# Second attention of a fused transformer kernel: value products of three steps a block divided in two, three buffers of probabilities

## The chip, the cores and the metric

One core of one Trainium2 chip runs the whole program in one launch. The metric is device time in microseconds (us). Five engines matter: TensorE (PE; its weight loads are shown as PEld), VectorE (DVE), ScalarE (ACT), GpSimd (POOL) and SyncE (SP), which issues most of the DMAs. Each runs its own list of instructions in order and meets the others only at semaphores.

## The reference, cut to what matters

The input x is 16 sequences of 256 tokens with 128 features. Four layers follow each other, each on the layer norm of x and each added to x: an attention with 2 heads, a gated feed-forward, a second attention with 16 heads of 8 features, and the same feed-forward again. The change is in the second attention:

```python
qkv = encodings @ attn_w.T + attn_b            # 16 heads, 8 features each
scores = einsum('bhki,bhqi->bhkq', k, q) / math.sqrt(8)
scores = where(mask, scores, -10000.0)         # a key is seen by itself and later queries
probs = softmax(scores, axis=2)                # over the keys
combined = einsum('bhkq,bhkl->bhql', probs, v)
out = combined.transpose(...).reshape(b, n, 128) @ out_w.T + out_b
```

## The kernel before

**Blocks and steps.** The second attention goes through 8 blocks of 2 sequences (512 tokens). A block has 8 steps (`STEPS`, L1300); step n handles one sequence (n % 2) and one group of 4 heads (n // 2). The 4 heads are two pairs, p = 0 and p = 1. Blocks 1 to 4 are the two rounds of a loop whose semaphore targets stand in registers (`run_inner`, L256); blocks 0, 5, 6 and 7 are written out.

**Two passes over the scores.** For block b+1 a first pass (`pe_first`, L1339) makes the scores with queries on the partitions, and DVE takes the row maximum of each (`dve_first`, L1665). The maxima are transposed on PE (`pe_maxT`, L1360), copied and negated on ACT (`act_max`, L1580) and carried by a DMA from the ACT queue into the operand rows of the queries (`act_max_rows`, L1586). For block b a second pass (`pe_second`, L1373) makes the scores with keys on the partitions, the maximum already taken off, and leaves them in one pair of PSUM banks for both pairs of heads. ACT takes the exponential out of these banks into a buffer of probabilities in SBUF (`act_exp`, L1563), POOL zeroes the masked half of the diagonal tiles (`pool_mask`, L1781), and the value products (`pe_values`, L1393) multiply the probabilities by the values, 16 columns of weights a head (8 values and a column of ones that sums the denominator), the 4 heads in four column strips of the array.

**The value products of a step.** There are two key tiles. Key tile 0 (kc = 0) meets all 256 queries, key tile 1 (kc = 1) only the last 128, and accumulates on them. In fp32 each product is two passes on PE, so a step has 8 passes of 256 columns and 8 of 128.

**The order on PE, step n** (`pe_step`, L1424): second pass of pair 0; first pass of pair 1 of block b+1, which ends in two mask products (L1357); a small piece of other work (`pe_between`, L1464); second pass of pair 1; first pass of pair 0; value products of step n−1. Below, the part from the second pass of pair 0 is the step's A half and the part from the second pass of pair 1 its B half; each begins by waiting until ACT has emptied the two banks (semaphore `s_ex`). The small pieces are: step 0 `pe_maxT` of the block's upper half, step 1 the transposes of the layer norm, 2 and 3 the q and k projections of block b+2, 4 and 5 half of the v projection each, 6 `pe_maxT` of the next block's lower half, 7 the output projection of block b−1, which waits for POOL's normalisation (L1792).

**Buffers of probabilities.** There are two, used in turn (`prob[n % 2]`). ACT waits before the exponential of step n until the value products of step n−2 are done (`s_pv`, L1569).

**Order on ACT:** exponential of pair 0; `act_max` at steps 0 and 6; exponential of pair 1; at steps 0, 2, 4, 6 the copy of the output bank (`act_out`, L1574), which waits for the value products of the odd step before.

**The loads of the rows.** The q and k of block b+2 go through DRAM. SP (`sp_body`, L1893) stores the q rows, then the reciprocals of the denominators that DVE makes at the end of step 3 (`dve_inverse`, L1682), then the k rows; once these have landed it issues the load of the lower half of the rows (L1866), which the first pass of step 0 of the next block waits for (L1344). The second pass of step 0 waits for the DMA of the maxima (L1428).

Of the kernel before, what the change touches and what calls it, by code (L numbers as in the profile page):

```python
# [24 lines left out]
P = 128  # L25
B, T, E = 16, 256, 128
# [17 lines left out]
GROUPS = 4  # L44
QUART = P // GROUPS
# [35 lines left out]
def is_block(b, t):  # L81

    return isinstance(b.t, int) and b.t == t


def build(nc, io):
    ctx = ExitStack()
    with ctx:
        scope = [ctx]

        def sb(name, shape, dt=F32):
            return scope[-1].enter_context(nc.sbuf_tensor(name, shape, dt))

        def sem(name):
            return ctx.enter_context(nc.semaphore(name))
# [135 lines left out]
        def mm(out, lhsT, rhs, start=True, stop=True):  # L231
            return nc.tensor.matmul(out, lhsT, rhs, start=start, stop=stop)  # L232
# [14 lines left out]
        def wait(engine, semaphore, value):  # L247

            if not isinstance(value, int) or value > 0:
                engine.wait_ge(semaphore, value)  # L250

        LAST = BLOCKS - 1
# [985 lines left out]
        def attention_b(link):  # L1238
# [10 lines left out]
            REP = 2 * DB  # L1249
            PAIRS, HALVES = 2, 2  # L1250
            qs, ks = h_split
            va, prob = b_values, b_prob
# [16 lines left out]
            o_bank = banks3[:, 2, :]  # L1269
# [18 lines left out]
            s_pv = sem("b_values_weighted")  # L1288
# [11 lines left out]
            STEPS = SEQS * GROUPS  # L1300
# [2 lines left out]
            MAX1_AT, T_AT, Q_AT, K_AT, V_AT, MAX0_AT, OUT_AT = 0, 1, 2, 3, 4, 6, 7  # L1303
            INVERSE_AT, NORMALISE_AT, STATS_AT = 3, 6, 6
            GATE_AT = {2: 0, 4: 1, 6: 2}
            HEAD_PAIR = 1
            LOADS = 16 * 2
            STORES = 16 * 6

            def group(n):  # L1310

                return n // SEQS, n % SEQS
# [80 lines left out]
            def pe_values(pe, b, n):  # L1393
                g, s = group(n)
                if is_block(b, LAST):
                    return pe_values_in_parts(pe, b, n)
                pe.wait_ge(s_ms, UNITS * b.t + PAIRS * (n + 1))
                if s == 0:
                    wait(pe, s_oc, GROUPS * b.t + g)
                if n == 0:  # L1400
                    pe.wait_ge(s_vr, b.t + 1)
                for kc in range(2):
                    for j in range(GROUPS):
                        pr = prob[n % 2][:, j // 2, :, j % 2, :]
                        last = mm(o_bank[QUART * j:QUART * j + REP, s * T + kc * P:(s + 1) * T],
                                  va[b.odd][:, 2 * s + kc, g * GROUPS + j, :],
                                  pr[:, 1:2, :] if kc else pr[:, 0:3:2, :], start=kc == 0, stop=kc == 1)
                last.then_inc(s_pv, 1)

            def pe_values_in_parts(pe, b, n):  # L1410
                g, s = group(n)
                if s == 0:
                    pe.wait_ge(s_oc, GROUPS * b.t + g)
                for p, done in ((0, s_pv0), (1, s_pv)):
                    pe.wait_ge(s_ms, UNITS * b.t + PAIRS * n + p + 1)
                    for kc in range(2):
                        for j in (2 * p, 2 * p + 1):
                            pr = prob[n % 2][:, p, :, j % 2, :]
                            last = mm(o_bank[QUART * j:QUART * j + REP, s * T + kc * P:(s + 1) * T],
                                      va[b.odd][:, 2 * s + kc, g * GROUPS + j, :],  # L1420
                                      pr[:, 1:2, :] if kc else pr[:, 0:3:2, :], start=kc == 0, stop=kc == 1)
                    last.then_inc(done, 1)

            def pe_step(pe, b, n, before, one, two, parts=None):  # L1424
                prev, nxt = link["prev"], link["next"]
                n1, n2 = b.after(1), b.after(2)
                if n % HALF == 0:
                    pe.wait_ge(s_ml[n // HALF][b.odd], 16 * (b.pair + 1))  # L1428
                if is_block(b, 0) and n == 0:
                    for slot in range(2):  # L1430
                        pe.wait_ge(prev["hi_written"][slot], 4 * BLOCKS)
                pe_second(pe, b, n, 0)
                if one:
                    pe_first(pe, n1, n, (1,))
                if is_block(b, 0) and n == 0:
                    prev["pe_tail"](pe, parts, 0)
                if one:
                    pe_between(pe, b, n, before, two)
                pe_second(pe, b, n, 1)
                if one:  # L1440
                    pe_first(pe, n1, n, (0,))
                if is_block(b, 0) and n == 1:
                    pe.wait_ge(prev["done"], BLOCKS)
                if not one and n > 2:
                    if n == 3:
                        pe.wait_ge(nxt["split_written"], 1)
                    for _ in range(2):
                        mm(misc[:, :], ident_b[:, :], mask[:, :, :].rearrange("p g k -> p (g k)"))
                if n:
                    pe_values(pe, b, n - 1)  # L1450
                elif before:
                    pe_values(pe, b.after(-1), STEPS - 1)
                if not one and n == MAX1_AT:
                    pe.wait_ge(s_nm, HALVES * b.t + 1)
                    pe_maxT(pe, b, 1)
                if is_block(b, 0) and n == 0:
                    prev["pe_tail"](pe, parts, 1)
                if not one and n == T_AT:
                    pe.wait_ge(s_nm, HALVES * BLOCKS)
                    nxt["pe_T"](pe, FIRST_BLOCK)  # L1460
                if not one and n in GATE_AT:
                    nxt["pe_gate"](pe, FIRST_BLOCK, GATE_AT[n], parts, HEAD_PAIR)

# [29 lines left out]
            def pe_body(pe, b, before, one, two, parts=None):  # L1493
                for n in range(STEPS):
                    pe_step(pe, b, n, before, one, two, parts)
                if not one:
                    pe_values(pe, b, STEPS - 1)
# [39 lines left out]
            def pe_last(pe, parts):  # L1537

                nxt = link["next"]
                pe_body(pe, LAST_BLOCK, True, False, False, parts)  # L1540
                nxt["pe_gate"](pe, FIRST_BLOCK, KC - 1, parts, HEAD_PAIR)
                pe.wait_ge(nxt["split_written"], 1)
# [20 lines left out]
            def act_exp(act, b, n, p):  # L1563
                act.wait_ge(s_p2, UNITS * b.t + PAIRS * n + p + 1)
                if is_block(b, LAST) and n > 1:
                    act.wait_ge(s_pv if p else s_pv0, n - 1 + (STEPS * b.t if p else 0))
                elif p == 0:

                    wait(act, s_pv, STEPS * b.t + n - 1)  # L1569
                nc.scalar.activation(prob[n % 2][:, p, :, :, :],  # L1570
                                     second_banks(b, p)[:, :, 0:3 * P].rearrange("p b (c q) -> p c b q", c=3), ACT.Exp,
                                     scale=SCALE_B).then_inc(s_ex, 1)

# [18 lines left out]
            def act_body(act, b, before, one, two):  # L1592
                prev, nxt = link["prev"], link["next"]
                n1, n2 = b.after(1), b.after(2)
                for n in range(STEPS):
# [26 lines left out]
                    if not one and n == T_AT:  # L1622
                        act.wait_ge(s_pv, STEPS * LAST)
                        nxt["act_xhi"](act, FIRST_BLOCK)
                    if not one and n in GATE_AT:
                        nxt["act_tanh"](act, FIRST_BLOCK, GATE_AT[n], HEAD_PAIR)
                if not one:
                    act_out(act, b, GROUPS - 1)
                    nxt["act_tanh"](act, FIRST_BLOCK, KC - 1, HEAD_PAIR)
                    nxt["act_xhi"](act, SECOND_BLOCK)  # L1630
# [61 lines left out]
            def dve_body(dve, b, before, one, two):  # L1692
# [4 lines left out]
                for n in range(STEPS):  # L1697
# [29 lines left out]
                    if not one and n == T_AT:  # L1727
                        nxt["dve_xlo"](dve, FIRST_BLOCK)
                        nxt["norm"].dve_stats(dve, SECOND_BLOCK)
                    if not one and n in GATE_AT:  # L1730
                        nxt["dve_gate"](dve, FIRST_BLOCK, GATE_AT[n], HEAD_PAIR)
                        nxt["dve_hlo"](dve, FIRST_BLOCK, GATE_AT[n])
                    if before and n == INVERSE_AT:
                        dve_inverse(dve, b.after(-1))
                if not one:
                    nxt["norm"].dve_apply(dve, SECOND_BLOCK, False)
                    dve_down(dve, b.after(-1))
                    nxt["dve_gate"](dve, FIRST_BLOCK, KC - 1, HEAD_PAIR)
                    nxt["dve_hlo"](dve, FIRST_BLOCK, KC - 1)
# [39 lines left out]


            def pool_mask(pool, b, n, p):  # L1781
                pr = prob[n % 2][:, p, 0:2, :, :].rearrange("p c b q -> p (c b) q")
                pool.wait_ge(s_ex, UNITS * b.t + PAIRS * n + p + 1)
                pool.sem_inc(s_turn, 1)

                nc.gpsimd.affine_select(out=pr, in_=pr, compare_op=ALU.is_ge, fill=0.0, base=0,  # L1786
                                        pattern=[[0, 4], [1, P]], channel_multiplier=-1).then_inc(s_ms, 1)
# [155 lines left out]
        scope.pop().close()  # L1943
        scope.append(ExitStack())
        b_values = [sb(f"b_values{i}", [P, TILES, HB, 2 * DB]) for i in range(2)]
        b_prob = [sb(f"b_prob{i}", [P, 2, 3, 2, P]) for i in range(2)]
        scope.pop().close()
        xn_split["f2"], g1_split["f2"] = ffn_inputs("f2")
        links = [{"prev": None, "next": None} for _ in range(4)]
# [132 lines left out]
```

## Time and profile before

| | us |
|---|---|
| runs shown | 693.09, 695.62, 697.49 |
| median | 695.62 |
| the profiled execution, its own time | 692.88 |
| its span, first to last instruction | 691.1 |
| PE busy | 641.8 (93%) |
| DVE busy | 470.6 (68%) |
| ACT busy | 443.6 (64%) |
| POOL busy | 423.5 (61%) |
| second attention, steps of blocks 1 to 6 | 147.02 |

The mean granted TensorE clock was 0.992. Busy time says how much of the span an engine had an instruction in work; it does not say that the engine set the pace in that stage. A busy PE also includes the time in which a pass is in the pipeline and the next one has not started. In a timeline row the columns are the start, the time to the end of the group, engine, line, operation, output <- input, tile (rows*columns of the array), shape, count, and in brackets the idle time before it with what ended it. The rows and columns of PE that are named f_h_hi and f_h_lo are the q and k rows of the attention (the buffers are shared with the feed-forward).

### The profile page before, as it was taken

How to read it: one execution, taken by the hardware profiler on the slowest of the kernel's cores; microseconds unless marked ns; L12 is line 12 of the kernel's file. 1: busy time of each engine (PE TensorE's matmuls, PEld its weight loads, DVE VectorE, ACT ScalarE, POOL GpSimd, SP SyncE). 2: the span in 40 equal slices, each digit the busy share in tenths (PEclk: the TensorE clock that was granted, in tenths of full speed). 3: DMA queues.
4: the chain of work that ended last, by engine and by line, in shares of the span. 5: the costliest groups of instructions: out<-in, count | busy, mean ns of one | idle time of the engine just before them, and what ended most of it. 6: DMA issues, size and time to landing. Idle time of an engine off the chain costs nothing.

```text
span 691.1 us, 14147 instructions
## 1 busy us (share of the span) xinstructions
PE 641.8 (93%) x4764; PEld 452.6 (65%) x4764; DVE 470.6 (68%) x925; ACT 443.6 (64%) x781; POOL 423.5 (61%) x456
## 2 busy tenths in 40 slices
PE   3799997999999999998999999998889999999997
PEld 2456665777787786664555555555457777787785
DVE  6477777855677587466888888877577755677511
ACT  3688877665656664555767767766755665656664
POOL 4455455677777766442464564555547876777773
PEclk9999999999999999998999999999999999999999
DMA  6333234000000002631666666662220000000001
GB/s 198 78 85 96 64 76 50 1 1 1 0 0 0 1 1 92 220 118 58 220 192 224 211 220 214 225 223 86 83 94 18 2 15 16 15 15 0 17 16 31
DMA packets 35588, 56.60 MB, mean 82 GB/s; under 512 B 5072, under 2 KB 10192, under 8 KB 35536
## 3 DMA queue, kind: packets, MB, share of 16 engines
q1 hardware_dynamic: 35344, 55.66, 26.4%
q8 instruction: 30, 0.49, 0.3%
q10 hardware_dynamic: 192, 0.26, 0.1%
q14 instruction: 22, 0.18, 0.1%
HBM read 27.08 MB, written 24.38 MB: 74 GB/s over the span
## 4 chain that ended last, share of the span: by engine, by line
PE 64%; ACT 7%; DVE 6%; issue 4%; DMA 3%; POOL 0%; ACTq 0%; SPq 0%; DVEq 0%; POOLq 0%
PE banks L232 61%; ACT b_prob L1570 4%; DVE xn L185 2%; PE banks L1017 1%; PE banks L224 1%; DVE f_gate L1132 1%; DMA b_o_dram<-b_o 1%; DMA f_h_lo<-b_k_dram 1%; DVE f_hidden L1139 1%; ACT f_g_hi L1088 1%; DVE f_h_hi L1136 1%; DMA f_h_hi<-b_negative_max 1%; DMA b_k_dram<-b_k_lo 1%; PE banks L1365 1%; ACT f_tanh L1079 0%
## 5 line engine op out<-in xcount | busy, mean ns | idle before, releaser
L1203 POOL TENSOR_TENSOR f_g_lo<-f_gelu,f_g_hi 128x512 fp32r<-128x512 f32 x127 | 162.8, 1291 | 53.3 <-ACT f_g_hi L1088 52.7
L1087 ACT ACTIVATE f_gelu<-banks,cols 128x512 f32<-128x512 f32 x128 | 88.3, 690 | 127.1 <-PE banks L232 105.1
L1669 DVE TENSOR_REDUCE b_segment_max<-banks 128x6 f32<-128x768 f32 x128 | 120.1, 950 | 28.1 <-PE banks L232 27.6
L1786 POOL TENSOR_SCALAR_AFFINE_SELECT b_prob<-b_prob 128x512 f32<-128x512 f32 x128 | 81.8, 640 | 91.2 <-ACT b_prob L1570 90.5
L232 PE MATMUL banks<-f_g_hi,whi 128*128 128x512 f32 x320 | 130.4, 407 | 2.2 <-POOL f_g_lo L1203 1.7
L232 PE MATMUL banks<-f_g_lo,whi 128*128 128x512 f32 x320 | 126.7, 396 | 0.0
L1570 ACT ACTIVATE b_prob<-banks 128x768 f32<-128x768 f32 x128 | 102.4, 807 | 37.5 <-PE banks L232 37.2
L1196 POOL TENSOR_TENSOR f_h_lo<-f_hidden,f_h_hi 128x512 fp32r<-128x512 f32 x60 | 77.6, 1293 | 58.3 <-DVE f_hidden L1139 50.5
L232 PE MATMUL banks<-f_h_hi,whi 128*128 128x512 f32 x256 | 104.1, 407 | 2.8 <-ACT f_g_hi L1088 2.0
L232 PE MATMUL banks<-f_h_lo,whi 128*128 128x512 f32 x256 | 101.4, 396 | 0.0
L1088 ACT ACTIVATE f_g_hi<-banks,cols 128x512 fp32r<-128x512 f32 x128 | 87.4, 683 | 0.0
L1132 DVE SCALAR_TENSOR_TENSOR f_gate<-f_tanh,banks 128x512 f32<-128x512 f32 x64 | 43.3, 676 | 47.2 <-ACT f_tanh L1079 47.2
L232 PEld LDWEIGHTS banks<-f_g_hi,whi 128*128 128x128 f32 x320 | 60.3, 188 | 18.0 <-POOL f_g_lo L1203 3.9
L232 PE MATMUL banks<-f_xn_split,whi 128*128 128x512 f32 x256 | 71.0, 399 | 0.3 <-DVE f_hidden L1139 0.3
L232 PEld LDWEIGHTS banks<-f_g_lo,whi 128*128 128x128 f32 x320 | 60.3, 189 | 13.2 <-issue 0.2
L185 DVE TENSOR_SCALAR xn<-X,mv,rstd 128x128 f32<-128x128 f32 (+1 forms) x96 | 67.5, 769 | 0.6 <-POOL rstd L219 0.4
L232 PEld LDWEIGHTS banks<-f_h_hi,f_h_lo 32*128 32x128 f32 x512 | 37.3, 185 | 44.4 <-ACT b_prob L1570 34.4
L232 PE MATMUL banks<-f_h_hi,f_h_lo 32*128 32x256 f32 (+1 forms) x512 | 55.5, 301 | 9.5 <-ACT b_prob L1570 6.8
L232 PEld LDWEIGHTS banks<-f_h_hi,whi 128*128 128x128 f32 x256 | 48.2, 188 | 18.8 <-issue 3.9
L232 PE MATMUL banks<-b_prob,b_values 128*16 128x256 f32 (+1 forms) x1024 | 55.8, 331 | 1.2 <-ACT b_o L1578 0.7
L232 PEld LDWEIGHTS banks<-f_xn_split,whi 128*128 128x128 f32 x256 | 47.6, 188 | 13.2 <-issue 1.2
L232 PEld LDWEIGHTS banks<-f_h_lo,whi 128*128 128x128 f32 x256 | 48.2, 188 | 11.2 <-issue 0.5
(127 smaller groups left out, 1047.6 us busy)
## 6 DMA issues: line engine op xcount, KB each, us to landing
f_h_hi<-b_q_dram SPq DMA_DIRECT2D x16, 512.0 KB, 4.1
f_h_lo<-b_k_dram SPq DMA_DIRECT2D x16, 512.0 KB, 5.2
b_o_dram<-b_o SPq DMA_DIRECT2D x8, 1024.0 KB, 4.4
b_q_dram<-b_q_hi SPq DMA_DIRECT2D x16, 256.0 KB, 3.2
b_k_dram<-b_k_hi SPq DMA_DIRECT2D x16, 256.0 KB, 2.9
w_stage<-in_wF SPq DMA_DIRECT2D x8, 352.0 KB, 3.4
b_q_dram<-b_q_lo SPq DMA_DIRECT2D x8, 256.0 KB, 3.4
b_k_dram<-b_k_lo SPq DMA_DIRECT2D x8, 256.0 KB, 3.3
```

What stands on the lines that cost most here:

```text
L185: nc.vector.tensor_scalar(xn[:, s, :], X[:, bass.ds(TILES * t + s, 1), :], mv[:, s, 0:1], rstd[:, s:s + 1], ALU.subtract, ALU.mult).then_i ...
L224: last = nc.tensor.transpose(bank[:, s * P:(s + 1) * P], xn[:, s, :], ident[:, :])
L232: return nc.tensor.matmul(out, lhsT, rhs, start=start, stop=stop)
L1017: last = nc.tensor.transpose(y_bank[:, s * P:(s + 1) * P], yT[:, s * P:(s + 1) * P], ident[:, :])
L1087: nc.scalar.activation(gf[c % 2][:, :], z_bank[c % 2], ACT.Gelu, scale=scale).then_inc(s_gf, 1)
L1088: nc.scalar.activation(hi[:, c, :], z_bank[c % 2], ACT.Gelu, scale=scale).then_inc(s_ghi[c % 2], 1)
L1132: nc.vector.scalar_tensor_tensor(out=uu[slot][:, :], in0=th[slot][:, :], scalar=1.0, in1=a[:, :], op0=ALU.add, op1=ALU.mult).then_inc(s_u, 1)
L1196: nc.gpsimd.tensor_tensor(hlo[n.odd][:, c, :], hf[c % 2][:, :], hhi[n.odd][:, c, :].bitcast(F32), ALU.subtract).then_inc(s_hlo[c % 2], 1)
L1203: nc.gpsimd.tensor_tensor(lo[:, c, :], gf[c % 2][:, :], hi[:, c, :].bitcast(F32), ALU.subtract).then_inc(s_glo[c % 2], 1)
L1570: nc.scalar.activation(prob[n % 2][:, p, :, :, :], second_banks(b, p)[:, :, 0:3 * P].rearrange("p b (c q) -> p c b q", c=3), ACT.Exp, scal ...
L1669: nc.vector.reduce_max(seg[:, g, s, 2 * p:2 * p + 2, :], first_pass[:, 2 * p:2 * p + 2, 0:3 * P].rearrange("p b (c k) -> p b c k", c=3), A ...
L1786: nc.gpsimd.affine_select(out=pr, in_=pr, compare_op=ALU.is_ge, fill=0.0, base=0, pattern=[[0, 4], [1, P]], channel_multiplier=-1).then_in ...
```

## The change

In steps 2, 4 and 6 of a block the four products of key tile 1 are left out where they stood, at the end of the following step, and are issued one half later: after the first pass of pair 1 and ahead of the small piece in step 4, in step 6, and in step 0 of the next block (for step 6). Blocks 0 to 6 do so; the last block (7) keeps its own order, and takes only the piece that block 6 left. The probabilities now have three buffers, in the order 0, 1, 2, 1; the exponential of an even step waits for the value products of step n−4 instead of n−2. No instruction of another engine is added, removed or moved.

```diff
+            PROB_OF = (0, 1, 2, 1)
+            HALVED = (2, 4, 6)
...
-                for kc in range(2):
-                    for j in range(GROUPS):
-                        pr = prob[n % 2][:, j // 2, :, j % 2, :]
-                        last = mm(o_bank[QUART * j:QUART * j + REP, s * T + kc * P:(s + 1) * T],
-                                  va[b.odd][:, 2 * s + kc, g * GROUPS + j, :],
-                                  pr[:, 1:2, :] if kc else pr[:, 0:3:2, :], start=kc == 0, stop=kc == 1)
-                last.then_inc(s_pv, 1)
+                pe_values_of(b, n, 0)
+                if n not in HALVED:
+                    pe_values_of(b, n, 1).then_inc(s_pv, 1)
+
+            def pe_values_of(b, n, kc):
+
+                g, s = group(n)
+                for j in range(GROUPS):
+                    pr = prob[PROB_OF[n % 4]][:, j // 2, :, j % 2, :]
+                    last = mm(o_bank[QUART * j:QUART * j + REP, s * T + kc * P:(s + 1) * T],
+                              va[b.odd][:, 2 * s + kc, g * GROUPS + j, :],
+                              pr[:, 1:2, :] if kc else pr[:, 0:3:2, :], start=kc == 0, stop=kc == 1)
+                return last
...
                 if is_block(b, 0) and n == 0:
                     prev["pe_tail"](pe, parts, 0)
+                if n == 0 and before:
+                    pe_values_of(b.after(-1), STEPS - 2, 1).then_inc(s_pv, 1)
+                elif n - 2 in HALVED and not is_block(b, LAST):
+                    pe_values_of(b, n - 2, 1).then_inc(s_pv, 1)
                 if one:
                     pe_between(pe, b, n, before, two)
...
-                    wait(act, s_pv, STEPS * b.t + n - 1)
-                nc.scalar.activation(prob[n % 2][:, p, :, :, :],
+                    wait(act, s_pv, STEPS * b.t + n - (1 if n % 2 else 3))
+                nc.scalar.activation(prob[PROB_OF[n % 4]][:, p, :, :, :],
...
-        b_prob = [sb(f"b_prob{i}", [P, 2, 3, 2, P]) for i in range(2)]
+        b_prob = [sb(f"b_prob{i}", [P, 2, 3, 2, P]) for i in range(3)]
```

## Rows read from the trace of the kernel before

**Rows 1.** Windows: one block, from its first second pass to the next block's.

```profile
362.78:387.33 24.55, 23.72 (x325) 14.32 (x321) 20.65 (x38) 17.57 (x25) 13.79 (x21) 1.00 0.66 219
```

**Rows 2.** Waits between 336 and 485 us: total us, times, longest.

```profile
PEld banks L232 <- ACT b_prob L1570: 31.1, 82, 1.0
```

**Rows 3.** Timeline of PE, block 2: end of step 5 and A half of step 6.

```profile
380.13 0.39 PE L232 MATMUL banks<-b_mask,b_ident 128*128 128x256 bf16 x2
380.45 0.84 PE L232 MATMUL banks<-b_prob,b_values 128*16 128x256 f32 x16
381.22 0.38 PE L232 MATMUL banks<-f_h_hi,f_h_lo 32*128 32x256 f32 x2
381.24 0.38 PE L232 MATMUL banks<-f_h_lo,f_h_hi 32*128 32x256 f32 x2
...
381.61 0.39 PE L232 MATMUL banks<-b_mask,b_ident 128*128 128x256 bf16 x2
381.84 0.60 PE L1365 MATMUL banks<-ident,b_max 128*8 128x128 f32 x4
382.65 0.38 PE L232 MATMUL banks<-f_h_hi,f_h_lo 32*128 32x256 f32 x2 [0.21 <-ACT b_prob L1570]
```

**Rows 4.** Timeline of PE, cut inside the value products of step 4.

```profile
380.89 0.40 PE L232 MATMUL banks<-b_prob,b_values 128*16 128x128 f32 x8
```

**Rows 5.** Timeline of PE, last block: value products ahead of full transposes.

```profile
488.37 0.86 PE L232 MATMUL banks<-b_prob,b_values 128*16 128x256 f32 x16
489.16 0.66 PE L224 MATMUL banks<-ident,xn 128*128 128x128 f32 x4
```

**Rows 6.** Timeline of ACT, block 2, steps 3, 5 and 6.

```profile
374.23 0.80 ACT L1570 ACTIVATE b_prob<-banks 128x768 f32<-128x768 f32 x1
...
380.13 0.81 ACT L1570 ACTIVATE b_prob<-banks 128x768 f32<-128x768 f32 x1 [0.54 <-PE banks L232]
381.78 0.81 ACT L1570 ACTIVATE b_prob<-banks 128x768 f32<-128x768 f32 x1 [0.84 <-PE banks L232]
382.56 0.59 ACT L1584 ACTIVATE b_negative_max<-banks 8x512 fp32r<-8x512 f32 x1
383.13 0.81 ACT L1570 ACTIVATE b_prob<-banks 128x768 f32<-128x768 f32 x1
```

**Rows 7.** Timeline of PEld, block 2, second passes of step 4.

```profile
375.15 0.33 PEld L232 LDWEIGHTS banks<-f_h_hi,f_h_lo 32*128 32x128 f32 x4 [0.34 <-issue]
...
376.60 0.18 PEld L232 LDWEIGHTS banks<-f_h_hi,f_h_lo 32*128 32x128 f32 x2 [0.20 <-ACT b_prob L1570]
```

**Rows 8.** Timeline of PE, step 0 of blocks 2 and 3.

```profile
362.78 0.44 PE L232 MATMUL banks<-f_h_hi,f_h_lo 32*128 32x256 f32 x4
363.04 0.44 PE L232 MATMUL banks<-f_h_lo,f_h_hi 32*128 32x256 f32 x4
...
387.33 0.44 PE L232 MATMUL banks<-f_h_hi,f_h_lo 32*128 32x256 f32 x4
388.14 0.44 PE L232 MATMUL banks<-f_h_lo,f_h_hi 32*128 32x256 f32 x4 [0.37 <-DMA f_h_lo<-b_k_dram]
...
388.75 0.60 PE L1365 MATMUL banks<-ident,b_max 128*8 128x128 f32 x4
```

**Rows 9.** Timeline of DVE, block 2, end of step 3.

```profile
375.90 0.54 DVE L1685 RECIPROCAL b_den_inv<-b_den 128x64 f32<-128x64 f32 x1
```

**Rows 10.** Timeline of SP, block 2: reciprocals stored, rows loaded.

```profile
376.47 0.34 SPq L1887 DMA_DIRECT2D b_inv_dram<-b_den_inv  x1
...
382.40 0.47 SPq L1866 DMA_DIRECT2D f_h_lo<-b_k_dram  x1
```

**Rows 11.** The load's line (L1866) in 382.0 to 382.5 us: time to landing.

```profile
DMA to landing us min/median/max: 4.0/4.8/5.6
```

**Rows 12.** Timeline of ACT, block 3, step 0.

```profile
389.46 0.59 ACT L1584 ACTIVATE b_negative_max<-banks 8x512 fp32r<-8x512 f32 x1 [0.76 <-PE banks L1365]
389.96 0.78 ACT L1570 ACTIVATE b_prob<-banks 128x768 f32<-128x768 f32 x1
```

More of the change, by code:

```diff
@@ L1417, in pe_values_in_parts @@
                         for j in (2 * p, 2 * p + 1):
-                            pr = prob[n % 2][:, p, :, j % 2, :]
+                            pr = prob[PROB_OF[n % 4]][:, p, :, j % 2, :]
                             last = mm(o_bank[QUART * j:QUART * j + REP, s * T + kc * P:(s + 1) * T],
@@ L1781, in pool_mask @@
             def pool_mask(pool, b, n, p):
-                pr = prob[n % 2][:, p, 0:2, :, :].rearrange("p c b q -> p (c b) q")
+                pr = prob[PROB_OF[n % 4]][:, p, 0:2, :, :].rearrange("p c b q -> p (c b) q")
                 pool.wait_ge(s_ex, UNITS * b.t + PAIRS * n + p + 1)
```

## The prediction

> **What bounds the kernel now.** I read the windows by block first, then the waits of the stage, then the timelines of PE, ACT, DVE and SP over one block. A block takes 24.55 us and PE is busy for 23.72 of them [rows 1]; but the busy share hides that PE's weight loads waited 82 times, 31.1 us in all, for an exponential [rows 2]. So the pace is set half by half: a half ends when both PE has issued its work and ACT has emptied the two banks. The reader is to see three things.
>
> First, which side ends a half. The second pass of step 6 starts at 381.22 right behind the value products, while the exponential it needs ended at 380.13 + 0.81 = 380.94 [rows 3, 6]: that B half is bound by PE, by some 0.22 us (a released second pass starts 0.06 after the exponential, 381.78 + 0.81 = 382.59 against 382.65). The A half of step 6 runs from 381.22 to 382.65, 1.43 us, and ends on the exponential: PE was idle [rows 3].
>
> Second, a longer loop lies over the halves. At step 0 the first pass (388.14) starts 0.81 us behind the second pass (387.33), released by the load of the k rows; in block 2 it starts at 363.04 against 362.78 [rows 8]. Without a wait the two start 0.02 apart (381.22 and 381.24 [rows 3]). The same late start is there in blocks 2 to 6, five times. The load was issued at 382.40 and took 5.6 us to land, 388.0 [rows 10, 11]. SP had come to it from the store of the reciprocals (376.47), which waited for DVE's reciprocal at the end of step 3, 375.90 [rows 9, 10]. So from the end of step 3 (375.90) to the first pass of the next step 0 (388.14) 12.2 us pass in DMAs, whatever PE does in steps 4 to 7, as long as PE gets there earlier. What lies between that first pass and the end of step 3 is fully exposed.
>
> Third, the exponential of step n never waited for a buffer: the value products of step n−2 stand ahead of the second pass of step n in PE's own order, so when the scores are there the buffer is free. The third buffer removes no wait; it only allows the later products.
>
> **The change, part by part.** *Taken out of a B half.* In steps 3, 5 and 7 the B half loses key tile 1. Its eight passes begin at 380.89, 0.44 after those of key tile 0 (380.45) [rows 3, 4], so a double pass of 256 columns takes 0.22 and one of 128 columns 0.11: 2 x 0.11 = 0.22 us saved on PE. What is gained is the smaller of this and the room to the exponential. Step 5: 0.22. Step 3: nothing, because its second exponential runs from 374.23 to 375.03 and the next second pass loads at 375.15, on ACT already [rows 6, 7]. Step 7: between 0 and 0.22, like its neighbours; I take 0.14 as an estimate, since its half starts without the wait that makes step 5's a little longer.
>
> *Put into an A half.* After the last mask product a full-array piece starts 0.23 behind the first mask product (381.61 to 381.84), value products 0.32 behind (380.13 to 380.45) [rows 3]: the column strips cost 0.09 more to enter. Then 2 x 0.11 for the passes and 0.02 for the four heads' spacing. Leaving them costs the same whether a second pass follows (0.77 from 380.45 to 381.22) or a full transpose (0.79 from 488.37 to 489.16) [rows 3, 5]: 0.20 from the last pass, instead of 0.11 between full pieces. Sum 0.09 + 0.22 + 0.02 + 0.09 = 0.42 us more PE work in the A half. So a moved piece costs PE 0.42 and saves 0.22.
>
> The Trainium skill, "TensorEngine Tiling (Array Packing)", section Key Properties, says that changing the tiling mode drains the TensorE, which speaks against this change, since each piece adds one more way in and out of the strips. The rows agree in direction. By the page the next product waits for the end of the one before; the value products' record ends 0.07 after the next start [rows 3, 4], so with a full drain ten exposed switches would add 0.7 us to the sum. The measured row decides.
>
> *Step 4.* The A half, 375.15 to 376.60, has PE idle about 0.08 to 0.19 of it (the weight loads show 0.20 [rows 7]): +0.24 to +0.34. In the loop blocks the next half then starts without a wait, which gives back 0.08. Net +0.2.
> *Step 6.* The maxima's transposes begin at 381.84; 3 x 0.11 and 0.20 later PE could start the next half, 382.37, 1.15 after 381.22. With the piece 1.57 (up to 1.66 when the half began on a wait), against 1.43: +0.14 to +0.23, as much as step 5 saved.
> *Queued behind.* `act_max` stands ahead of the second exponential on ACT and now waits for transposes that come 0.42 later. How that looks stands in block 3, step 0: transposes at 388.75, copy at 389.46, exponential at 389.96 [rows 8, 12], about 0.2 later behind its second pass than the 0.48 of step 6 (382.65 to 383.13 [rows 3, 6]). The B half is then bound below by 0.68 + 0.78 + 0.06 = 1.52 us on ACT, while PE's work in it is 1.4 to 1.6 (0.49 to the value products' mask, 0.32, 0.77): no cost, within 0.1. But the DMA of the maxima leaves later too.
> *Steps 4 to 7 in sum:* +0.2 − 0.22 + 0.2 − 0.14, about zero, and hidden under the 12.2 us of DMAs. Both ends of that estimate, 0.3 more or less, stay under the 0.81 of block 3; in block 2 the cover is 0.24 thin, and where it runs out PE sets the start again.
> *Step 0.* The piece stands behind the first pass, which the load releases. Five times (blocks 2 to 6) it is exposed, less the idle end of that A half, 0 to 0.06: 5 x 0.41 = 2.05 us. And the 0.14 that step 7 saved only lets PE wait earlier for the same load.
>
> *Ends of the chain.* Block 0 to block 1: the load is there in time, so steps 4 to 7 count: between 0.3 and 0.5, I take 0.4. Block 6 to block 7: no load follows, +0.2. The maxima's DMA, delayed by half a microsecond, may pass the load at one of the five: 0 to 0.5, I take 0.2. Nothing else moves: no DMA is issued or reordered, and all of it lies in the 147 us of this stage.
>
> **Sum:** 2.05 + 0.4 + 0.2 + 0.2 = 2.85, about +3 us. The profiled execution took 692.88 (span 691.1), so 695.9. It lies 0.4% under the median of the runs shown, 695.62; the same share on that median gives 698.6.
>
> **Rivals.**
> *A, slightly faster.* The switches cost nothing beside idle time and the load does not bind (it lands 4.0 us after issue for its first packets, 5.6 for the last [rows 11], so a little less traffic would do). Then per block step 5 gives 0.22, step 7 0.14, step 4's follower 0.08, and the A halves take nothing but 0.04: −0.4 x 7 = −2.8 us, 692.8. For it: the idle time in the A halves is real [rows 3, 7]. Against it: the extra 0.09 on either side is in the rows, and so is the late first pass in five blocks. No B half can give more than 0.22, so 21 x 0.22 = 4.6 us is the most that can be won: 691.0.
> *B, the load is not in the loop, the switches cost what I say.* Per block +0.2 (step 4), −0.22, +0.2, −0.14, +0.14 (step 0, 1.43 to 1.57): +0.2 x 7 = +1.4 us, 697.0.
> *C, clearly slower.* The maxima's DMA becomes the last release of step 0. It leaves behind the second exponential of step 6, which moves by step 4's +0.3 and step 6's own +0.4; it decides from the point where it lands after the row load, about 0.4 to 1 us later than now. Then steps 4 to 7 are exposed as well: 0.3 + 0.2 + 0.42 + 0.1 = 1.0 a boundary, 7 us, 702.6. Against it: at 388.14 it was the row load that came last, by 0.81 [rows 8].
> *D, it does not do what it says:* the later products wait for nothing and every count of `s_pv` keeps its order, so I see no way to that; the full cost with no cover, 21 x 0.42 = 8.8, would be 704.4.
>
> **Chances.** My forecast 0.60, own range 696 to 701 with the scatter of the runs (693.09 to 697.49); A 0.15; B 0.12; C 0.10; D or something unseen, a shift of code among it, 0.03. About 1% (7 us) is what a measurement of this kernel can tell from no change. Faster by over 1% would take more than the 4.6 us bound of A: 0.04. Slower by over 1%: half of C and D: 0.08. Within 1%: 0.88. The range reaches from A's 692.8 to just under C: 692.8 to 702.
>
> **What the profile after would show.** Right: in blocks 2 to 6 the first pass of step 0 still starts behind its second pass, the value products of 128 columns stand between the mask products and the maxima's transposes, and these are some 0.42 later behind the first pass; the block gets longer by 0.4; PE's wait at the end of the A halves of steps 0, 4 and 6 is gone, and a wait at the end of the B halves of steps 3, 5 and 7 has come. Wrong: blocks shorter than 24.55 us; transposes less than 0.3 later; the start of step 0 released by the maxima's DMA.

## The result, and the profile after

Twenty runs of each kernel: 696.57 us median after (694.02 to 704.25), 693.53 before (691.36 to 697.51). The ratio is 1.0055, 95% interval 1.0029 to 1.0080: slower by about half a per cent, within 1%. I had forecast +3.0 us on the median, a ratio of 1.0043, and a range of 692.8 to 702. The number was right. The reason given for it was right in part only, and the experiments show in which. Four of the twenty runs of the changed kernel took 702.9 to 704.3 us at a mean granted clock of 0.976 or 0.977; the other sixteen, at 0.988 to 0.994, have a median of 696.1 us, 2.6 above that of before, and a mean 2.3 above it.

The profiled execution has a span of 694.8 us against 691.1. Block 3 by the windows, from its first second pass to that of block 4, answers to [rows 1] (busy time and count of PE, PEld, DVE, ACT, POOL, then granted clock, DMA share, GB/s):

```profile
387.79:412.83 25.04, 24.24 (x321) 13.73 (x322) 21.13 (x38) 17.54 (x25) 13.84 (x20) 1.00 0.63 213
```

Blocks 1 to 4 last 25.04 to 25.06 us each, block 5 24.93; before they were 24.83, 24.55, 25.04, 24.55 and 24.40. They have become alike, but that says nothing about the division: in the kernel with three buffers and nothing divided (below) blocks 2 to 4 are alike too, at 24.54, 24.53 and 24.54 us. Block 3 was the longer one before because of one late load. Of the 3.7 us between the two spans, blocks 1 to 5 make 1.78 and block 6 makes 2.62 (26.28 against 23.66 us); block 0 gives back 0.80, since PE's clock stood at its 1.2 GHz level for 6.8 us at the start of the stage in the profiled execution before and for 3.4 in the one after. So the profiles alone can't give the price of the division; the halves can.

The timeline of PE over steps 4 to 6 of block 2 answers to [rows 3, 7]:

```profile
375.45 0.39 PE L232 MATMUL banks<-f_h_hi,f_h_lo 32*128 32x256 f32 x2 [0.30 <-ACT b_prob L1582]
375.56 0.39 PE L232 MATMUL banks<-f_h_lo,f_h_hi 32*128 32x256 f32 x2
...
375.94 0.39 PE L232 MATMUL banks<-b_mask,b_ident 128*128 128x256 bf16 x2
376.26 0.41 PE L232 MATMUL banks<-b_prob,b_values 128*16 128x128 f32 x8
376.60 0.71 PE L232 MATMUL banks<-wB,xnT 128*128 128x128 f32 x4
377.24 0.38 PE L232 MATMUL banks<-f_h_hi,f_h_lo 32*128 32x256 f32 x2
...
381.01 0.62 PE L232 MATMUL banks<-b_prob,b_values 128*16 128x256 f32 x8
381.57 0.38 PE L232 MATMUL banks<-f_h_hi,f_h_lo 32*128 32x256 f32 x2
...
382.04 0.39 PE L232 MATMUL banks<-b_mask,b_ident 128*128 128x256 bf16 x2
382.36 0.41 PE L232 MATMUL banks<-b_prob,b_values 128*16 128x128 f32 x8
382.70 0.60 PE L1367 MATMUL banks<-ident,b_max 128*8 128x128 f32 x4
383.23 0.39 PE L232 MATMUL banks<-f_h_hi,f_h_lo 32*128 32x256 f32 x2
```

The moved piece is the row of 128x128 x8. The A half of step 4 now lasts 377.24 − 375.45 = 1.79 us (1.42 before), that of step 6 383.23 − 381.57 = 1.66 (1.43), and neither ends on the exponential. The wait that moved stands at 375.45: the B half of step 3 lost its piece and got 0.30 us of idle time. From the first mask product to the transposes it is 0.66 (382.04 to 382.70) where it was 0.23 [rows 3]: 0.43 more, as forecast (0.42). The start of step 0 of blocks 3 and 6 answers to [rows 8]:

```profile
387.79 0.38 PE L232 MATMUL banks<-f_h_hi,f_h_lo 32*128 32x256 f32 x2
387.99 0.38 PE L232 MATMUL banks<-f_h_lo,f_h_hi 32*128 32x256 f32 x2
...
462.82 0.44 PE L232 MATMUL banks<-f_h_hi,f_h_lo 32*128 32x256 f32 x4 [0.30 <-DMA f_h_hi<-b_negative_max]
464.03 0.44 PE L232 MATMUL banks<-f_h_lo,f_h_hi 32*128 32x256 f32 x4 [0.77 <-DMA f_h_lo<-b_k_dram]
```

In block 3 there is no wait for the row load any more (it landed at 387.16, before the second pass; the 0.20 us between the two passes is there in block 1 too, where the load landed 2.7 us ahead), and yet the block is as long as the others. In block 6 both DMAs that I had named, the maxima's and the rows', were late one behind the other.

### The profile page after: what moved, and what is told of

The parts are those of the page before. It is cut to its first block, busy times and chain, and to the rows that moved or that the text cites. A ratio compares the mean times of both kernels' runs of the same rounds, so it can differ in the third digit from the quotient of the medians.

```text
span 694.8 us, 14146 instructions
## 1 busy us (share of the span) xinstructions
PE 646.2 (93%) x4764; PEld 449.1 (65%) x4764; DVE 471.0 (68%) x925; ACT 443.5 (64%) x781; POOL 423.8 (61%) x456
## 4 chain that ended last, share of the span: by engine, by line
PE 64%; DVE 7%; ACT 6%; issue 4%; DMA 2%; POOL 0%; SPq 0%; ACTq 0%; DVEq 0%; POOLq 0%
PE banks L232 61%; ACT b_prob L1582 3%; DVE xn L185 2%; PE banks L1017 1%; PE banks L1367 1%; PE banks L224 1%; DVE f_gate L1132 1%; DMA f_h_lo<-b_k_dram 1%; DMA b_o_dram<-b_o 1%; DVE f_hidden L1139 1%; ACT f_g_hi L1088 1%; DVE f_h_hi L1136 1%; DVE b_segment_max L1681 1%; DMA b_k_dram<-b_k_lo 1%; ACT f_tanh L1079 0%
## 5 line engine op out<-in xcount | busy, mean ns | idle before, releaser
L232 PE MATMUL banks<-b_prob,b_values 128*16 128x256 f32 (+1 forms) x1024 | 60.4, 334 | 0.9 <-POOL b_prob L1798 0.6
```

## The experiments

All ratios are against the kernel before, run beside it on the same chip. "Blocks 1 to 5" is the time from the first second pass of block 1 to that of block 6 in the profiled execution; it is 123.36 us before and 125.14 after. It is one execution for each kernel, so a late transfer or a low clock in it counts in full. In the expectations theory 1 is the predicted one, in which the load of the rows sets step 0 and hides what PE does in steps 4 to 7; in theory 2, the halves, every half counts for itself and the load seldom matters.

| kernel | ratio (95%) | blocks 1 to 5 |
|---|---|---|
| the change | 1.0055 (1.0029 to 1.0080) | 125.14 |
| three buffers, nothing divided | 1.0025 (1.0004 to 1.0046) | 122.72 |
| divided into step 0 only | 1.0033 (1.0019 to 1.0047) | 125.02 |
| divided into step 4 only | 1.0019 (1.0003 to 1.0035) | 124.47 |
| divided into step 6 only | 0.9996 (0.9980 to 1.0013) | 123.14 |
| piece behind the small piece | 1.0037 (1.0023 to 1.0050) | 125.34 |
| piece in the next B half | 1.0056 (1.0035 to 1.0078) | 124.23 |
| k rows stored first | 1.0099 (1.0074 to 1.0125) | 129.39 |
| row load issued late | 1.0078 (1.0060 to 1.0097) | 129.27 |
| step 6 only, behind | 0.9998 (0.9978 to 1.0018) | 122.45 |
| reciprocals stored by ACT | 1.0005 (0.9988 to 1.0022) | 122.84 |
| the same and step 6 only, behind | 1.0002 (0.9984 to 1.0020) | 126.95 |
| the same and the change | 1.0047 (1.0027 to 1.0067) | 127.02 |

**The buffers alone.**

```diff
-            HALVED = (2, 4, 6)
+            HALVED = ()
```

> Three buffers in the order 0, 1, 2, 1 and nothing divided. Every theory: the exponential never waited for a buffer, so 1.000 of before, within 0.3%; blocks 1 to 5 as long as before (24.4 to 25.0 us). A ratio away from 1 would mean that part of the loss is in the buffers or in the shifted code.

1.0025, and the lower end of the interval is just above 1. Two of its twelve runs took 699.20 and 698.81 us, at a mean granted clock of 0.975 and 0.984; the mean of the other ten is 693.95 against 693.80 before, and the halves are those of before. So the buffers and the shifted code cost nothing that shows in the halves, and a ratio here can be off by 0.2% through one or two such runs. It is also the cleanest reading of the undivided halves: blocks 2 to 4 take 24.54, 24.53, 24.54 us, where in the kernel before a late load lengthened block 3 (25.04).

**One moved piece at a time.** Three kernels, with

```diff
-            HALVED = (2, 4, 6)
+            HALVED = (6,)        # into step 0; (2,) into step 4; (4,) into step 6
```

In these kernels and in the one above, the piece of step 0 also got the condition that step 6 is in `HALVED`.

> Only step 6 is divided, so key tile 1 moves from step 7 to step 0 of the next block. Theory 1 (the predicted one: the row load's landing starts step 0, steps 4 to 7 are hidden under it): nearly the whole loss is here, +2.3 us (ratio 1.003), blocks 1 to 5 longer by 0.4 each. Theory 2 (the halves set the pace everywhere, the load only seldom): +0.3 for the A half of step 0 less 0.1 for the B half of step 7, about 0.2 a block, +1.4 us (1.002).

> Only step 2 is divided, so key tile 1 moves from step 3 to step 4. Theory 1: hidden under the 12.2 us of DMAs in blocks 1 to 5, exposed only in blocks 0 and 6, +0.4 us (1.0006); the next block's first step waits less for the load instead. Theory 2: step 4's A half +0.35, its B half -0.08, nothing won in step 3: +0.26 a block, +1.8 us (1.0026), blocks 1 to 5 longer by 0.26 each on the mean.

> Only step 4 is divided, so key tile 1 moves from step 5 to step 6. Both theories: B half of step 5 -0.22 (loop) or -0.14, A half of step 6 +0.24, B half of step 6 -0.06: 1.000, between -0.5 and +0.5 us. If the later maxima (their transposes about 0.4 later) are what costs, it is slower, +1 us or more, with the start of step 0 released by the DMA of the maxima.

Step 0: 1.0033, where theory 1 said 1.003 and the halves 1.002; the interval holds both, and the profiled execution had late loads in blocks 2, 3 and 6. Step 4: 1.0019, where theory 1 said 1.0006 and the halves 1.0026. Step 6: 0.9996. The timeline of PE in step 4 (block 2) of the second of them:

```profile
376.11 0.39 PE L232 MATMUL banks<-f_h_hi,f_h_lo 32*128 32x256 f32 x2 [0.31 <-ACT b_prob L1582]
...
376.92 0.41 PE L232 MATMUL banks<-b_prob,b_values 128*16 128x128 f32 x8
377.26 0.71 PE L232 MATMUL banks<-wB,xnT 128*128 128x128 f32 x4
377.90 0.39 PE L232 MATMUL banks<-f_h_hi,f_h_lo 32*128 32x256 f32 x2
```

The A half is 1.79 us again (1.42 before), the B half behind it 1.48 (1.56): +0.29. Blocks 2 to 5 are longer than those without division by 0.66, 0.31, 0.32 and 0.24, the first with a late load in it (0.67 us at its step 0). The intervals of the ratios alone don't tell theory 1 from the halves; the blocks do: a piece in step 4 is not hidden. The three deviations sum to 0.0048, the change has 0.0055.

**The place within the A half.**

```diff
-                if n == 0 and before:
-                    pe_values_of(b.after(-1), STEPS - 2, 1).then_inc(s_pv, 1)
-                elif n - 2 in HALVED and not is_block(b, LAST):
-                    pe_values_of(b, n - 2, 1).then_inc(s_pv, 1)
                 if one:
                     pe_between(pe, b, n, before, two)
+                if n == 0 and before:
+                    pe_values_of(b.after(-1), STEPS - 2, 1).then_inc(s_pv, 1)
+                elif n - 2 in HALVED and not is_block(b, LAST):
+                    pe_values_of(b, n - 2, 1).then_inc(s_pv, 1)
```

> The change, with the moved products behind the small piece of steps 4, 6 and 0 instead of ahead of it. The way from the small piece to the row tiles of the second pass costs 0.20 already, so only one more way into the strips is paid: 0.20 + 0.11 + 0.02 = 0.33 us more PE work instead of 0.42, and the maxima's transposes are not late any more. Halves theory: 0.1 a piece less than the change, and the B half after step 6 and 0 as before: +1 us against before (1.001 to 1.003), 2 us better than the change. If it is the later maxima that cost, it comes out at 1.000 or better. If the place does not matter: 1.0055 like the change.

1.0037: the runs can't tell it from the change. The halves can. Step 4 of block 4, timeline of PE:

```profile
427.49 0.39 PE L232 MATMUL banks<-f_h_hi,f_h_lo 32*128 32x256 f32 x2 [0.30 <-ACT b_prob L1582]
...
428.21 0.61 PE L232 MATMUL banks<-wB,xnT 128*128 128x128 f32 x4
428.75 0.41 PE L232 MATMUL banks<-b_prob,b_values 128*16 128x128 f32 x8
429.09 0.39 PE L232 MATMUL banks<-f_h_hi,f_h_lo 32*128 32x256 f32 x2
```

1.60 instead of 1.79 in step 4, 1.57 instead of 1.66 in step 6. From the v products to the second pass it takes 0.64 when they follow the strips (376.60 to 377.24) and 0.54 to the next piece when they follow the mask products (428.21 to 428.75): weights of 128 columns cost 0.1 more to bring in behind the strips than my transposes (8 columns) let me see. The profiled execution itself had two late loads (blocks 2 and 3), so its sum of blocks is no better than the change's.

**No more ways in and out.** The same four lines directly ahead of `pe_values` at the end of `pe_step`.

> The change, with the moved products another half later, directly ahead of the next value products in the B halves of steps 4, 6 and 0. No way into or out of the strips is added: PE's work is that of before. Halves theory: B halves of steps 3, 5, 7 give 0, 0.22, 0.14; those of 4, 6, 0 take 0.22 each less the small room they have: about +0.2 a block, +1.5 us (1.002), against +0.26 - 0.04 + 0.25 = 0.47 a block for the change. The difference to the change is the price of the switches.

The timeline of PE, B half of step 4 in block 4:

```profile
426.70 0.39 PE L232 MATMUL banks<-f_h_hi,f_h_lo 32*128 32x256 f32 x2
...
427.50 1.06 PE L232 MATMUL banks<-b_prob,b_values 128*16 128x128 f32 x24
428.49 0.38 PE L232 MATMUL banks<-f_h_hi,f_h_lo 32*128 32x256 f32 x2
```

24 passes in one row, and the half lasts 1.79 (1.57 before), exactly the 0.22 of four products. The A halves are those of before, and blocks 1 to 5 take 1.5 us more than undivided ones instead of 2.4. That is the price of the switches in the profile, 0.9 us in five blocks. The runs don't confirm it: 1.0056, no better than the change. The profiled execution (693.55 us) was one of two of the six runs, at a granted clock of 0.995 and 0.993; the other four took 696.4 to 698.5 at 0.983 to 0.989. So the mean holds time at the low clock that the profile doesn't show. What brought it was not traced.

**The chains of DMAs.** First SP's order in the kernel before, then a later load:

```diff
                 if before:
-                    sp_inverse_store(sp, n1, out_at)
                 if two:
                     sp_store_rows(sp, n2, rows_at, "k")
+                if before:
+                    sp_inverse_store(sp, n1, out_at)
```

> The kernel before; only SP's order is changed: the k rows are stored ahead of the reciprocals, so the row load is issued and lands 1 to 1.5 us earlier. Theory 1 (12.2 us of DMAs from step 3 to the next step 0 set the block): blocks 2 to 6 lose their whole wait at step 0, faster by 0.1 to 0.6 a block until another wait takes over, -1.5 us or more (0.998). Theory 2 (landing is just about in time, the halves set the pace): -0.3 to -0.8 us, within 0.1%.

```diff
+                if before and two:
+                    sp.wait_ge(s_il, out_at["stored"])
                 if two:
                     sp_load_rows(sp, n2, rows_at, False)
```

> The kernel before; SP issues the row load only after the inverse rows have landed, 0.6 to 1.3 us later than now. Theory 1: every block from 2 to 6 is longer by the whole delay, +3 to +5 us (1.006). Theory 2: the landing was late by some tenths in some blocks and early in others, so the delay is paid less what was in hand, +2 to +4 us (1.004). No effect (1.000) would mean that the load is never in the way.

Neither theory had the first right: 1.0099. The row load landed 0.9 to 1.7 us ahead of the second pass in blocks 2 to 6, and it brought nothing, because the other chain was now late. PE and POOL in block 1:

```profile
361.66 1.13 PE L232 MATMUL banks<-wB,b_oTn 128*128 128x128 f32 x8 [1.65 <-POOL b_oTn L1792]
```

```profile
360.25 1.26 POOL L1792 TENSOR_TENSOR b_oTn<-b_oT,b_inv 128x512 f32<-128x512 f32 x1 [1.84 <-DMA b_inv<-b_inv_dram]
```

The output projection of step 7 waits for POOL's normalisation, and this for the reciprocals. Their store did not only leave later, it also took longer: 3.2 to 4.6 us from issue to landing right behind the three stores of k rows, against 1.5 to 1.9 in blocks 2 to 4 before (3.5 and 2.5 in blocks 1 and 5). Each chain has next to nothing in hand. The late load says the same from the other side: 1.0078, +5.4 us for a load issued about 1 us later (its profiled execution also spent 10 us of this stage at the 1.2 GHz level, of which more below). In block 2 of it PE stood for 1.47 us:

```profile
362.31 0.44 PE L232 MATMUL banks<-f_h_hi,f_h_lo 32*128 32x256 f32 x4
364.23 0.69 PE L232 MATMUL banks<-f_h_lo,f_h_hi 32*128 32x256 f32 x4 [1.47 <-DMA f_h_lo<-b_k_dram]
```

**Both chains out of each other's way.** The store of the reciprocals goes to the ACT queue, in the kernel before, and then also in the changed one:

```diff
-                if before:
-                    sp_inverse_store(sp, n1, out_at)
...
                         act_max(act, n1, 0)
+                    if before and n == INVERSE_AT + 1:
+                        sp_inverse_store(act, b.after(-1), {"read": b.t})
                     act_exp(act, b, n, 1)
```

> The kernel before; the store of the reciprocals is issued from the ACT queue in step 4 instead of by SP, so SP can store the k rows about 1.3 us earlier and neither chain of DMAs delays the other. If the row load's landing is what makes step 0 late in some blocks, its first pass now starts 0.07 behind the second pass in all blocks, without the new wait at step 7 that the other order of SP brought: -0.7 to -1.5 us (0.998 to 0.999). If the k-first order was slower for another reason (its stores in each other's way), this is slower too, by 1% again.

> The changed kernel with the reciprocals stored from the ACT queue. Against the same edit on the kernel before this is the price of the division alone, with no landing in the way: halves theory +0.26 (step 4) -0.04 (5, 6) +0.25 (7, 0), 0.47 a block, +3.3 us (1.0045 above that kernel's ratio). If the change lost its time to the landing it would be less, 1.001 to 1.002 above.

The first removes the late loads. Step 0 of block 3 with the edit alone:

```profile
388.16 0.38 PE L232 MATMUL banks<-f_h_hi,f_h_lo 32*128 32x256 f32 x2
388.24 0.39 PE L232 MATMUL banks<-f_h_lo,f_h_hi 32*128 32x256 f32 x2
```

The first pass stands 0.07 to 0.08 behind the second pass in all of blocks 1 to 6: no row load is late, and the kernel is as fast as before, 1.0005. That alone does not decide, because the other chain was not left in peace: the store of the reciprocals now took 3.2 to 3.4 us to land in every block, and in block 3 POOL waited for them:

```profile
409.14 1.27 POOL L1794 TENSOR_TENSOR b_oTn<-b_oT,b_inv 128x512 f32<-128x512 f32 x1 [0.36 <-DMA b_inv<-b_inv_dram]
```

The A half of step 7 took 1.87 and 2.02 us in blocks 2 and 3, where it took 1.62 and 1.63 before. A gain at step 0 may have been lost there, and the interval leaves room for 0.8 us. What decides is the A half of step 0 itself. In blocks 2, 4 and 5 of the kernel before, the late first pass left it at 1.43, 1.43 and 1.39 us, the same as in the three-buffer kernel, where the loads were in time (1.43, 1.43, 1.40). Only block 3 paid (1.95) and block 6 a little (1.55 against 1.39 here). So the late starts of [rows 8] were not what set the pace.

The change costs 1.0047 with this edit too, so 0.0042 or 2.9 us over the same edit without it, and no row load is in the way. Its blocks 3 to 5 take 25.04, 25.07 and 25.09 us, about as in the change. But in blocks 1 and 2 of its profiled execution step 7 waited for the normalisation (A halves of 2.58 and 2.53 us, against 1.63 and 1.87), so some of the 2.9 us may be of that chain and not of the halves.

**Looking for a gain.** The place where halves gave something, step 6 behind the transposes, alone and with the ACT queue's store:

```diff
-            HALVED = (2, 4, 6)
+            HALVED = (4,)
```

> Only the place where the halves showed a gain: step 4 is divided, its key tile 1 goes to step 6, behind the maxima's transposes (a half with 0.2 to 0.28 us of idle PE). B half of step 5 -0.22 or -0.14, A half of step 6 +0.14, B half of step 6 -0.08 in the loop: about -0.1 a block, -0.8 us (0.999). Where the row load's landing sets step 0, even this is given back: 1.000.

> Both together: reciprocals stored from the ACT queue, and step 4 divided with its key tile 1 behind the transposes of step 6. With the landing out of the way the halves' gain is not given back: -0.8 us from the one and -1 from the other, 0.997. If the landing still sets step 0, no better than either alone.

0.9998 and 1.0002. In the profile of the first the pair of halves is shorter by 0.07 to 0.08 (B half of step 5 1.35 instead of 1.57, A half of step 6 1.57 instead of 1.43) and so is the B half of step 6, and blocks 3 and 4 take 24.36 and 24.37 us instead of 24.54. In blocks 0, 5 and 6 the pair gains nothing (B half of step 5 1.35 instead of 1.49, A half of step 6 1.49 instead of 1.35), so it would be 0.7 us in the four loop blocks or 0.1%, less than the intervals. No version here beats the kernel before by what can be measured. The second lost 2.4 us in block 1 of its profiled execution, where PE waited 1.39 us for the normalisation and then ran slower, so moving the store did not free that chain either: the store of the reciprocals took 4.4 us to land in that block.

## Why the prediction was right, and where it was not

- **The price of the piece: right.** 0.42 us forecast, 0.43 measured ahead of the transposes, 0.22 saved. A switch costs 0.09 on the way in and as much on the way out. Where 128 columns of weights follow it is 0.1 more, which I had not seen.
- **The drain of the Trainium skill** ("TensorEngine Tiling (Array Packing)", Key Properties) names the right sign: more switches, more time. The trace shows no full drain as far as its records go, whose ends are modelled: the transposes start at 382.70, 0.07 before the end of the piece's record (382.36 + 0.41).
- **What hides it: wrong.** "From the end of step 3 to the first pass of the next step 0 12.2 us pass in DMAs, whatever PE does in steps 4 to 7" failed. I took five late starts in one execution for a loop that sets the block. A half starts with its second pass and ends on the exponential, and a first pass that comes 0.2 us late costs it nothing (1.43 us either way); only two of the five late starts did. In blocks 2 to 5, in the nine executions with SP's own order and load, the last row landed anywhere from 0.74 us before the second pass to 0.96 after it; in block 6 it was late in eight of the nine, by 0.37 to 1.39 us. And [rows 11] was misread in rival A: 4.0 us is the load of the q rows and 5.6 that of the k rows behind it, not the first and the last packets of one load. A load that is later still is dear (1.0078); an earlier one would have given the two halves 0.7 us together in the profiled execution before (0.52 in block 3, 0.16 in block 6).
- **Step 4: mis-sized.** Forecast as hidden in five blocks. Measured +0.35 to +0.37 in the A half of the loop's blocks, with −0.08 in the B half behind it, and +0.44 to +0.47 in blocks 0, 5 and 6: 2.5 us over blocks 0 to 6; 1.0019 in the runs.
- **Steps 5 and 6: right.** −0.14 to −0.22 against +0.23 to +0.24: 0.9996.
- **Step 0: right in size, not in cause.** 2.05 forecast. Its A half grew by 0.26 to 0.34, less what step 7 gave back, which did count after all: about 1.5 us; 1.0033.
- **So the sum stood on errors that offset each other:** step 0 charged in full and step 4 not. By the halves the sum is about 2.5 + 0.1 + 1.5 = 4.1 us over blocks 0 to 6, 2.9 of it in blocks 1 to 5. Something did hide, though not what I had named, and less: in blocks 1 to 5 the waits for the normalisation at step 7 got shorter by 0.6 us (blocks 1 and 5) and the wait for the rows in block 3 by 0.5, which leaves the 1.8 that was measured. The ratio of the runs gives 3.8 us with the four runs at the low clock and 2.3 without them, the medians 3.0 and 2.6; I had said 3.0. That the forecast fell so near was luck.
- **The third buffer** removed no wait, as said. **Rival C** showed itself in one block: in block 6 the second pass waited 0.30 us for the maxima's DMA, which I had named as a sign of being wrong, and the first pass 0.77 for the rows. Rival B, the load not in the loop and the switches dear, was nearest to the mechanism; it got 0.12 and a sum of 1.4 us, too low because it charged step 4 with 0.2 (0.27 to 0.46 measured) and step 0 with 0.14 (0.26 to 0.34 measured in its A half).

## What to carry to other kernels

Work moved from a full half into one with idle time is worth only what the idle time holds after the cost of changing the array's tiling there and back; price the ways in and out from the rows, and put the piece at a border that exists already. A transfer that is seen late may be following the compute: ask first whether the stretch it starts late also ends late, and make the transfer early in an experiment before you build a sum on it. Where two chains of DMAs depend on each other's stores, look at both after you reorder them: the store of the reciprocals landed 3.1 us or more after its issue wherever it was put behind the stores of the k rows. And look at the clock of every run beside its time before you read a ratio of half a per cent.

## What the runs showed of the hardware

A wait of PE of about a microsecond or more can cost more than itself. Windows of the kernel with the late load (block 2, step 0), then of the changed kernel (block 6, step 0); the third number from the right is the granted clock:

```profile
362.30:364.30 2.00, 0.53 (x10) 0.37 (x6) 1.65 (x7) 0.81 (x1) 1.07 (x2) 0.98 1.03 376
364.30:367.00 2.70, 2.70 (x19) 1.73 (x20) 0.96 (x1) 0.61 (x2) 0.27 (x1) 0.50 0.58 211
367.00:370.00 3.00, 3.00 (x29) 1.49 (x29) 0.96 (x1) 1.82 (x3) 0.63 (x1) 0.50 0.02 5
```

```profile
463.00:466.00 3.00, 2.23 (x30) 1.24 (x29) 1.34 (x3) 1.10 (x2) 0.91 (x2) 0.98 0.92 301
466.00:469.00 3.00, 3.00 (x34) 1.26 (x28) 0.96 (x1) 1.84 (x4) 0.64 (x1) 0.50 0.11 42
```

PE was idle for 1.47 us and then ran at 0.50, the 1.2 GHz level, over the next two windows; block 2 took 29.33 us. In the changed kernel the value products of one step took 1.48 us where they take 0.84, after waits of 0.30 and 0.77 us, and block 6 took 26.28. The wait of 0.37 us in [rows 8] had no such effect. Nor does every long wait have it: in the kernel with the k rows stored first PE was idle for 1.65 us in block 1 and the clock stayed at 1.00 (361.7 to 370 us), while 1.72 us in block 5 of the same execution were followed by the low level.

It also happens in runs that were not profiled, since every run's mean granted clock is on record. The four runs of the changed kernel at 702.9 to 704.3 us had 0.976 or 0.977, the others 0.988 to 0.994; from these means, (0.992 − 0.977) x 702 us and twice that because the level is half the full clock, I estimate some 20 us more at 1.2 GHz. The 82 runs of the kernel before that stood beside the experiments had 0.986 or more and took 696.55 us at most. One run with three buffers and nothing divided had 0.975, so the division is not needed for it. Where in the four runs the clock fell is not known; block 6, where the row load was late in eight of nine profiled executions, is a candidate and no more.

The time to landing of one small store varied by a factor of three. That of the reciprocals took 1.5 us in blocks 3 and 4 of the kernel before, where it was issued ahead of the stores of the k rows, and 3.2 to 4.6 in all blocks of the two kernels that issued it behind them, from SP or from the ACT queue. In blocks 1 and 5 of the kernel before it took 3.5 and 2.5 without that, so the order is not the only thing that sets it, and no experiment took the order alone.
